# Scores taken on the context through a folded weight, with the W1 halves scaled on GpSimd and a new order of the attention blocks

## The reference

```
x = x + attention(layernorm(x), ctx)     # query = n Wq + bq, key = ctx Wk + bk, value = ctx Wv + bv
                                         # scores = query key^T / 16, softmax over the 512 keys
n = layernorm(x)
top 2 of 8 experts by softmax(n Wr^T), gates renormalised over the two
x = x + sum over the two of gate * (gelu(n W1[e]^T + b1[e]) W2[e]^T + b2[e])
x: (4, 512, 256)   ctx: (4, 512, 192)   W1: (8, 1024, 256)   W2: (8, 256, 1024)
```

## Time and profile before

| what | us |
|---|---|
| median of 3 runs (418.13 to 418.59) | 418.39 |
| the profiled execution | 418.75 |
| its span | 416.7 |
| first expert matmul | 187.51 |
| TensorE busy, share of the span | 359.1 (86%) |
| VectorE | 272.9 (66%) |
| ScalarE | 189.2 (45%) |
| GpSimd | 150.2 (36%) |

### The profile page before, as it was taken

How to read it: one execution, slowest core, us unless ns; L and a number is a source line. 1 busy time by engine, 2 the same in 40 slices (tenths; PEclk the granted TensorE clock), 3 DMA queues, 4 the chain that set the end, 5 groups by cost and what they waited for, 6 DMA issues and landing times.

```text
span 416.7 us, 8657 instructions
## 1 busy us (share of the span) xinstructions
PE 359.1 (86%) x2630; PEld 276.4 (66%) x2630; DVE 272.9 (66%) x760; ACT 189.2 (45%) x323; POOL 150.2 (36%) x148
## 2 busy tenths in 40 slices
PE   7999889797979776008999989999999999999990
PEld 2445547453654455006888878889888899889870
DVE  1326675869586957766668987666766776677570
ACT  0346665665486535464433323334325434443420
POOL 4722240316255752803034644322223213312412
PEclk9999999899989996657899999999999999999996
DMA  7960336233843573542132348333363424444222
GB/s 216 383 189 2 101 112 230 101 101 112 281 151 101 148 212 124 173 104 104 27 52 67 89 57 96 51 44 52 40 55 52 52 40 67 52 41 65 29 25 25
DMA packets 51306, 41.93 MB, mean 101 GB/s; under 512 B 28673, under 2 KB 46721, under 8 KB 51137
## 3 DMA queue, kind: packets, MB, share of 16 engines
q1 hardware_dynamic: 39648, 26.31, 24.3%
q0 software_dynamic: 7872, 11.77, 15.9%
q10 hardware_dynamic: 3744, 3.31, 2.4%
HBM read 22.41 MB, written 13.86 MB: 87 GB/s over the span
## 4 chain that ended last, share of the span: by engine, by line
PE 63%; DVE 14%; issue 6%; ACT 6%; DMA 5%; POOL 3%; SPq 0%; POOLq 0%; ACTq 0%; DVEq 0%
PE o_ps L761 20%; PE s_ps L743 12%; PE t_ps L743 10%; PE s_ps L624 5%; PE proj L590 4%; DVE w2l L1063 3%; PE o_ps L643 3%; PE proj L582 2%; PE proj L611 2%; POOL rows L501 2%; PE proj L657 2%; DMA staged<-W2T 2%; POOL out L540 1%; PE t_ps L634 1%; ACT w2l L831 1%
## 5 line engine op out<-in xcount | busy, mean ns | idle before, releaser
L540 POOL DMA_INDIRECT out<-y,xm x39 | 61.5, 1577 | 127.7 <-DVE y L1317 119.0
L761 PE MATMUL o_ps<-w2h,gl 128*128 x312 | 85.0, 273 | 0.0
L761 PE MATMUL o_ps<-w2h,gh 128*128 x312 | 85.0, 272 | 0.0
L761 PE MATMUL o_ps<-w2l,gh 128*128 x312 | 85.0, 273 | 0.0
L938 ACT ACTIVATE g<-s_ps,b_sb,down 128x256 f32<-128x256 f32 (+1 forms) x96 | 44.5, 526 | 84.4 <-PE s_ps L743 84.4
L1290 DVE TENSOR_SCALAR gh<-g,up 128x512 f16<-128x512 f32 x78 | 39.1, 502 | 39.5 <-ACT g L938 37.9
L1292 DVE SCALAR_TENSOR_TENSOR gl<-g,up,gh 128x512 f16<-128x512 f32 x78 | 58.7, 752 | 2.8
L938 ACT ACTIVATE g<-t_ps,b_sb,down 128x256 f32<-128x256 f32 (+1 forms) x88 | 41.5, 533 | 38.5 <-PE t_ps L743 38.5
L743 PE MATMUL s_ps<-xT,w1h 128*128 128x256 f16 (+1 forms) x384 | 53.0, 265 | 6.8 <-DVE w2l L1063 5.7
L743 PE MATMUL t_ps<-xT,w1h 128*128 128x256 f16 (+1 forms) x352 | 47.5, 260 | 0.0
L743 PEld LDWEIGHTS s_ps<-xT,w1h 128*128 x384 | 34.9, 101 | 11.9 <-issue 7.2
(11 more groups left out here) (186 smaller groups left out, 556.3 us busy)
## 6 DMA issues: line engine op xcount, KB each, us to landing
staged<-W1T SPq DMA_DIRECT2D x8, 1024.0 KB, 5.7
staged<-W2T SPq DMA_DIRECT2D x8, 1024.0 KB, 6.6
rows<-send POOLq DMA_DIRECT2D x8, 260.0 KB, 5.8
out<-x_sb ACTq DMA_DIRECT2D x4, 512.0 KB, 6.5
w2l<-ctxT SPq DMA_DIRECT2D x4, 256.0 KB, 4.7
x_sb<-x SPq DMA_DIRECT2D x2, 512.0 KB, 6.1
x_sb<-x ACTq DMA_DIRECT2D x2, 512.0 KB, 5.9
b_sb<-b SPq DMA_DIRECT2D x1, 1024.0 KB, 4.8
```

The source lines that it names most:

```text
L540: pool.indirect_dma_start(out=out, out_offset=bass.IndirectOffsetOnAxis(ap=xm[:, t % MB, r, META - 1:META].bitcast(I32), axis=0), in_=y2[: ...
L761: i = nc.tensor.matmul(y_ps[n % 2][:, 0:D], l[:, t % 2, m, r * P:(r + 1) * P], w[:, bass.ds(e, 1), m * D:(m + 1) * D].rearrange("p a n -> ...
```

## The change

The keys are no longer made. Wq times Wk (turned, with bk as one more column, 193 in all) is multiplied once at the start (`fold`), the queries are taken through that product, and the scores are the product of these 193 numbers with the context itself, which has a row of ones for the bias. The scores' contraction is thus split into 128 and 65 rows where it was 128 and 128. The value bias comes in through the same row of ones, and `add_bv` on GpSimd is gone. The context has two buffers, x three.

The high halves of W1 (even units) are made on GpSimd, those of W2 stay on ScalarE. The sums of an expert's two matrices go through TensorE and the scale operations together: 8 chains where there were 16. The first eight units rotate over four staging places and the last eight over three. `low` is written as two instructions, of half a unit each. All orders inside a block are new.

More of the change, by code:

```diff
@@ L379, in _ @@
+            load_unit(2)
+            load_unit(3)
             load_ctx(1)
-            for u in range(RING, UNITS):
-                if u % QT == 1 and u // QT + 1 < B:
-                    load_ctx(u // QT + 1)
+            load_unit(4)
+            load_x(2)
+            load_unit(5)
+            load_ctx(2)
+            for u in range(6, UNITS):
+                if u == 9:
+                    load_x(3)
+                if u == 10:
+                    load_ctx(3)
                 load_unit(u)
@@ L589, in values @@
                     for t in range(2):
-                        i = nc.tensor.matmul(bank[:, 0:D], ctx_sb[0:part[t], t, k * P:(k + 1) * P],
-                                             wv_sb[0:part[t], t, :], start=(t == 0), stop=(t == 1))
+                        i = nc.tensor.matmul(bank[:, 0:D], ctx_sb[b % 2][0:PART[t], t, k * P:(k + 1) * P],
+                                             wv_sb[0:PART[t], t, :], start=(t == 0), stop=(t == 1))
                     i.then_inc(proj_full, 1)
@@ L607, in queries @@
                 taken(("xt", b, 1))
-                for c in range(DC):
+                for c in range(2):
                     bank = begin(("q", b, c))
                     for t in range(DC):
-                        i = nc.tensor.matmul(bank[:, 0:LQ], wq_sb[:, t, c * P:(c + 1) * P], normT[:, t, :],
+                        i = nc.tensor.matmul(bank[0:PART[c], 0:LQ], a_sb[:, t, c * P:c * P + PART[c]], normT[:, t, :],
                                              start=(t == 0), stop=(t == DC - 1))
@@ L675, in ranks @@
                 i.then_inc(proj_full, 1)
-            def add_all(u):
-                pe.wait_ge(squared, u + 1)
-                bank = begin(("sum", u, 0))
-                nc.tensor.matmul(bank[:, 0:2], ones32[:], sq[:, u, :], start=True, stop=True).then_inc(proj_full, 1)
-            keys(0)
-            pe.wait_ge(w_in, 48)
+            def add_all(e):
[3 more added lines that the diff above has]
+                                 start=True, stop=True).then_inc(proj_full, 1)
+            pe.wait_ge(consts, 1)
+            fold()
+            turn_x(0)
+            taken(("a", 0, 0))
+            taken(("a", 0, 1))
+            queries(0)
+            pe.wait_ge(wv_in, 32)
+            pe.wait_ge(ones_row, 2)
             values(0)
-            pe.wait_ge(consts, 1)
-            turn_x(0)
-            queries(0)
             pe.wait_ge(wr_in, 16)
             pe.wait_ge(b1q_ready, 1)
+            pe.wait_ge(qb_ready, 1)
             for b in range(B):
                 last = b == B - 1
-                u = QT * b
                 scores(b, 0)
@@ L709, in _ @@
                 if not last:
-                    keys(b + 1)
+                    queries(b + 1)
                 turn_probs(b, 3)
+                if b:
+                    ranks(b - 1)
                 attend(b, 2)
-                if not last:
-                    add_all(u + 1)
-                    turn_x(b + 1)
-                else:
-                    ranks(b - 1)
+                add_all(2 * b + 1)
                 attend(b, 3)
@@ L847, in queries @@
             def queries(b):
-                for c in range(DC):
-                    take(("q", b, c), qT[:, c, :], bank_of("q", b, c)[:, 0:LQ], bias=bqs_sb[:, c:c + 1], scale=SCALE)
+                for c in range(2):
+                    take(("q", b, c), qT[0:PART[c], c, :], bank_of("q", b, c)[0:PART[c], 0:LQ],
+                         bias=qb_sb[0:PART[c], c:c + 1], scale=SCALE)
             def turned_rows(name, b):
@@ L1058, in scale @@
+                link(nc.vector.tensor_scalar(power[:, both, :], bound[:, both, :].bitcast(I32), 24, None, ALU.logical_shift_right))
+                nc.vector.tensor_scalar(up[:, both, :], power[:, both, :], -2.0 ** 23, 205 * 2.0 ** 23, ALU.mult,
                                         ALU.add).then_inc(scale_ready, 1)
+                link(nc.vector.tensor_scalar(down[:, both, :], power[:, both, :], 2.0 ** 23, 49 * 2.0 ** 23, ALU.mult, ALU.add))
             def low(u):
-                dve.wait_ge(high_ready, u + 1)
+                dve.wait_ge(high1_ready if u % 2 == 0 else high2_ready, u // 2 + 1)
@@ L1126, in route_places @@
                 nc.vector.tensor_copy(place[:, b, :, :], place_sum[:]).then_inc(gate_ready, 1)
[L1128 to L1138 removed]
+            for k in range(2):
+                nc.vector.memset(ctx_sb[k][TXT2:TXT2 + 1, 1, :], 1.0).then_inc(ones_row, 1)
```

257 lines of the change are left out of this document (111 added, 146 removed).

## The result

| | before | after |
|---|---|---|
| median, us | 418.32 (4 runs) | 446.68 (4 runs, 444.97 to 446.83) |
| first expert matmul | 187.51 | 215.99 |
| from there to the end of the span | 229.2 | 228.6 |
| TensorE busy, share of the span | 359.1 (86%) | 361.8 (81%) |

The ratio is 1.067 (1.064 to 1.070). The forecast was 419.6, with a range from 408 to 428. The whole difference, 28.4 us, lies ahead of the first expert matmul (28.5).

A forecast was written before the change was run, and what follows sets the result against it. No engine is full, so a block is as long as its chain of waits, TensorE nearest. Blocks and tail summed to the first expert matmul at 188.7 against 187.5, +1.2 us: 419.95 profiled, 419.6 median; range 408 to 428.

The forecast's parts named there:

- the product's price on GpSimd: W1's high halves on GpSimd, 2048 elements a partition: 2.1 us each with the handoff, between 2.0 and 4.3.
- hidden behind layernorm 1 and the residual, until they pass 3 to 4 us: GpSimd products of units 0, 4, 8 and 12 are off the path unless each takes over 3 to 4 us.
- Rival E: GpSimd and VectorE block each other; a product waits one 1.2 us low piece, 4.8 over four: 424.4, chance 0.10.
- Rival D: GpSimd product at the two-input rate, 4.3 us; four on the path cost 2.15 more each: 428.2, chance 0.12.
- The walk: Block-by-block sum of priced operations through the first stage, ending with the first expert matmul at 188.7 us.
- the first low half of blocks 1 to 3: VectorE's first low half in these blocks, priced like any low half at 2.4 us in two pieces.
- The tail: From the fourth row maximum of block 3, at 152.2, to the first expert matmul: 36.5 us.
- the ring: Three places for units 8 to 15: ScalarE's squares wait for W2 loads in blocks 2 and 3, 5 us and more each.
- no gain at the start: Kernel start: the fold replaces keys but inputs must land first, so scores of batch 0 stay at 23.5 us.
- experts untouched: The expert stage after the first stage keeps its 229 us.
- rows, not weights, as the last thing to come: End of the first stage: rows bound the first expert matmul at 188.7; weights are ready earlier, about 180.
- Rival C: A 65-row score half costs what a 128-row one does; nine tiles at 0.3 each, 2.7: 416.9, chance 0.15.

The follow-up runs named there:

- experiment 5: The changed kernel with GpSimd's product for W1's high halves replaced by a plain cast of 1.89 us, factor left out; ratio 1.015 (1.008 to 1.022).
- Experiment 6: The changed kernel with casts for GpSimd's products of units 0, 4, 8, 12 alone, ratio 1.053, or of units 2, 6, 10, 14 alone, 1.043.
- experiment 8: The changed kernel, all high halves on ScalarE, plus dead key products (repeat 0.975), longer scale chains (0.990), or squares moved behind the queries (0.989).

## Why the prediction was wrong

**The step that failed** is the product's price on GpSimd, "so I take 2.1", bounded by 2.0 and 4.3 from a cast and from an operation with two inputs. It measured 5.44, beyond the 3 us at which the forecast called itself wrong. It stands four times in the sum as forecast: 4 times 3.34 is 13.4 us. The rest came from the next step: the products of units 0, 4, 8 and 12 as "hidden behind layernorm 1 and the residual, until they pass 3 to 4 us". The sum has the apply there at 1.3, as if nothing ran beside it, and it took 6.53, 6.51 and 6.76 for 1.38, so three blocks lose 15.7 in all. Together 29.1, and the forecast missed by 27.1. With the cast's length both terms shrink by 25 us in all (four times 3.55, three times 3.59); experiment 5 gave 22. Experiment 6 shows that both groups pay, with shares in its traces near these; its times leave them less certain.

**Rival E was dismissed for a wrong reason.** It had the right mechanism, at 1.2 us a time, and was put aside because "on the path they follow one another, not side by side". The order put three products beside applies and a fourth beside the small addition at 199.77. The Trainium skill's "SBUF — State Buffer", in "Who interferes with whom", was read for its rule on two SBUF inputs alone; the same list says that VectorE's `tensor_scalar` in a 2-port mode takes the pair as well, and that the later one blocks fully. The trace agrees, with 6.53 for 1.38. Rival D had the right sign and place and too small a price.

**The walk, with the right prices, is close.** It had first maxima at 55.9 and 90.9, exponentials of batch 3 at 139.6 and the fourth maximum at 152.2. Measured were 63.68, 108.03, 164.33 and 180.39. Three blocks at 8.5 more (5.1 for an apply, 3.3 for a product) make 64.4, 107.9 and 165.1, and the last of the four is off by 2.7. One price more was wrong and, as far as the trace shows, cost nothing: the first low half of blocks 1 to 3, at 2.4 in the walk, stands beside `split_rows` and takes 4.35, 4.34 and 4.34 (VectorE, GpSimd), for 2.47 elsewhere, while GpSimd's addition takes 3.19 for 2.12 alone; but the third row maximum, behind it, still waited 0.6 us and more for TensorE.

```profile
64.88 4.35 DVE L1081 SCALAR_TENSOR_TENSOR w2l<-w2l,up,w2h 128x1024 f16<-128x1024 f32 x2
...
64.96 3.19 POOL L513 TENSOR_TENSOR send<-xn,send 128x1024 f16<-128x1024 f32 x1
```

The tail, 36.5, took 35.6 with 3.3 more for the last product in it, so it was priced 4.2 too dear: above all, the first expert matmul stands 5.9 us behind the end of GpSimd's last transfer (210.05), not 8.6, since SyncE issued at 212.55.

**Right:** the ring. The squares wait for loads of W2 three times, 28.6 us in all (ScalarE's waits up to 216 us: total, times, longest; the first line is the exponentials'):

```profile
ACT probs L839 <- DVE negmax L1039: 36.5, 8, 7.4
ACT w2l L854 <- DMA staged<-W2T: 28.6, 3, 12.0
```

**Right:** no gain at the start (scores of batch 0 at 23.02 for 23.47), experts untouched, and rows, not weights, as the last thing to come: the first expert matmul's wait ends with their load (TensorE's timeline):

```profile
215.99 1.03 PE L769 MATMUL s_ps<-xT,w1h 128*128 128x256 f16 x4 [18.53 <-DMA xT<-rows]
```

**Rival C was right on the score tiles.** The chain that ended last (start, us, what):

```profile
23.02 3.44 PE s_ps L654 x8
27.11 1.84 PE s_ps L654 x4
...
67.03 3.63 PE s_ps L654 x4
```

Two tiles take 3.44, so 1.72 each as before, and one takes 3.63 at a granted clock of 0.50, the lower level. The keys' 2.01 is what 64 rows cost, and it doesn't carry over to 65 (experiment 8); taking it over made the sum 2.7 us too long. The rule of "TensorE: Matmul & The Clock Gate" (the Trainium skill, "Why this matters for your kernels"), that a matmul on few rows takes the time of one on 128, held for 65 rows and not for 64. What sets 64 apart is open.

**Unsettled:** of the 7.5 us that remain with the cast, 2.9 go to a late start, which may be one execution's, and 5.1 to the three applies; the tail came shorter than priced, so something else in the blocks is still unaccounted for. What keeps the keys' 12 us from counting in some executions of one kernel and not in others was not found.

## What to carry to other kernels

Price an operation by a row of its own form on its own engine; a cast and a two-tensor operation on GpSimd did not enclose the one-tensor product, and where no row of the form exists the bound has to stay open at the top. Before work goes to GpSimd, list what VectorE does meanwhile: here applies (6.53 us for 1.38), additions on four numbers (5.06 for 0.17) and low halves (4.35 for 2.47) waited for GpSimd's instruction, so for them "hidden beside" was "added to". And the engine that does an operation fastest isn't the place for all of it: 1.29 us on VectorE won the early blocks, 2.0 us on ScalarE the late ones.

## What the runs showed of the hardware

- On GpSimd, 128x2048 from float32 to float16: 5.44 us with a factor from memory, 5.37 with a constant, 3.59 as a product of two tensors, 1.89 as a cast; 0.92 us for 256 columns, so pieces are dearer. The same product takes 1.29 us on VectorE and 2.0 us on ScalarE.
- VectorE's apply waits for the length of GpSimd's instruction. A piece of it takes 0.39 to 0.41 us alone and, in the mean, 0.55 beside instructions of 0.92 us, 0.81 beside one of 1.89 us and 1.72 beside one of 5.44 us.
- Small VectorE operations of 8.3 us in all cost 9.6 us of time, while 12 us more of TensorE's products cost some 3.4 in one run and, in two executions of four of another, nearly all of it.
- A float32 pass of 512 columns took 592 ns with 128 and with 65 rows, 641 ns with 64.
